# Moving a light feed-forward layer from the second stage of a decoder kernel into its routing iterations

## The reference, cut to what matters

```python
x = x + attn(layernorm(x))
x = x + xattn(layernorm(x), ctx)
n = layernorm(x)                                    # xn3 in the kernel
light = gelu(rms_norm(n) * gamma_l @ w1_l + b1_l) @ w2_l + b2_l      # 512 -> 256 -> 512
s = n @ routing_token
b = -relu(s)
for _ in range(50):                                 # one chain of small steps
    a = 0.1 * log(8) - 0.1 * logsumexp((s + b) / 0.1)
    b = -relu(s + a)
scores = exp((s + a + b) / 0.1);  idx = top_k(scores, 512)
heavy[idx] = gelu(rms_norm(n[idx]) * gamma_h @ w1_h + b1_h) @ w2_h + b2_h   # 512 -> 2048 -> 512
x = x + light + heavy
```

## Time and profile before

| | |
|---|---|
| median of 3 runs | 4434.32 us (4433.23 to 4436.21) |
| profiled execution | 4434.12 us, its span 4432.4 us |
| mean granted TensorE clock | 0.957 of full speed |
| busy, share of the span | PE 92%, DVE 55%, ACT 47%, POOL 60% |
| first stage | ends at about 3104 us |
| second stage | 3104 to 4004 us |
| third stage | 4004 us to the end; routing iterations 4012 to 4122 us |

### The profile page before, as it was taken

One profiled execution on the slowest core, in us unless ns is written; L12 is line 12 of the kernel. 1 busy time (PEld: TensorE's weight loads), 2 busy tenths in 40 slices (PEclk: granted clock), 3 DMA queues, 4 the chain that ended last, 5 costly groups with the idle time before them and its releaser, 6 DMA issues. The chain is left out here.

```text
span 4432.4 us, 59161 instructions
## 1 busy us (share of the span) xinstructions
PE 4057.6 (92%) x18676; PEld 2174.1 (49%) x18676; DVE 2456.1 (55%) x3293; ACT 2075.7 (47%) x3407; POOL 2676.4 (60%) x1343
## 2 busy tenths in 40 slices
PE   8969999999999999999999999997589888883599
PEld 6734444444444444444444444443466666662244
DVE  3336666666666666666666666662266666652400
ACT  2214555655555555555555555554244444441110
POOL 1006888888888888888888888888222222220100
PEclk9968999999999999999999999999799999995799
DMA  6521322322222342122223223220311111112100
GB/s 193 151 68 52 79 57 55 97 57 52 84 71 55 112 116 57 53 82 72 55 55 97 57 52 91 62 53 20 112 51 54 47 55 52 47 33 89 38 10 10
DMA packets 340399, 299.90 MB, mean 68 GB/s; under 512 B 188779, under 2 KB 230251, under 8 KB 339304
## 3 DMA queue, kind: packets, MB, share of 16 engines
q1 hardware_dynamic: 272360, 275.94, 21.9%
q10 hardware_dynamic: 66048, 16.78, 1.7%
q0 software_dynamic: 1920, 6.29, 0.5%
HBM read 117.71 MB, written 64.54 MB: 41 GB/s over the span
## 5 line engine op out<-in xcount | busy, mean ns | idle before, releaser
L239 POOL TENSOR_TENSOR acc<-acc,probs 128x1024 f32<-128x1024 f32 x896 | 2132.4, 2380 | 312.7 <-ACT probs L642 179.7
L729 DVE TENSOR_REDUCE maxes<-ps 128x1 f32<-128x1024 f32 x1024 | 1250.8, 1221 | 709.0 <-PE ps L465 704.1
L645 ACT ACTIVATE probs<-ps,far_bias 128x1024 f32<-128x1024 f32 (+7 forms) x1280 | 1020.4, 820 | 989.0 <-DVE near_s L746 519.2
L500 PE MATMUL ps<-probs,v_head 128*64 128x512 f32 x4096 | 994.6, 606 | 2.3 <-ACT ctx_out L628 2.2
L465 PE MATMUL ps<-stacks 64*128 64x512 f32 x2048 | 761.1, 452 | 33.3 <-DVE maxes L729 32.0
L480 PE MATMUL ps<-stacks 64*128 64x512 f32 x1792 | 671.4, 449 | 0.0
L479 PE MATMUL ps<-stacks 128*128 128x512 f32 x2048 | 625.5, 419 | 2.9 <-ACT probs L642 2.2
L480 PEld LDWEIGHTS ps<-stacks 64*128 64x128 f32 x1792 | 271.7, 184 | 528.7 <-issue 367.2
L500 PEld LDWEIGHTS ps<-probs,v_head 128*64 128x64 f32 x4096 | 248.7, 136 | 483.8 <-issue 480.1
L479 PEld LDWEIGHTS ps<-stacks 128*128 128x128 f32 x2048 | 347.7, 188 | 228.5 <-issue 163.6
L746 DVE TENSOR_TENSOR near_s<-ps,near_bias 128x384 f32<-128x384 f32 (+2 forms) x576 | 285.0, 495 | 284.8 <-PE ps L480 261.6
(11 more groups left out here) (221 smaller groups left out, 4967.4 us busy)
## 6 DMA issues: line engine op xcount, KB each, us to landing
stacks<-c_k SPq DMA_DIRECT2D x128, 256.0 KB, 2.4
stacks<-c_q SPq DMA_DIRECT2D x128, 256.0 KB, 2.6
stacks<-c_d SPq DMA_DIRECT2D x256, 128.0 KB, 2.5
scr_v<-c_k ACTq DMA_DIRECT2D x32, 512.0 KB, 3.9
stacks<-c_q SPq DMA_DIRECT2D x128, 128.0 KB, 2.5
v_head<-scr_v SPq DMA_DIRECT2D x32, 512.0 KB, 3.7
sums<-scr_inv SPq DMA_DIRECT2D x128, 128.0 KB, 2.9
scr_ctx<-ctx_out SPq DMA_DIRECT2D x128, 128.0 KB, 2.3
```

Of the source, the lines that this page charges most:

```text
L239: pool.tensor_tensor(acc[:, qb, :], acc[:, qb, :], pr, ALU.add).then_inc(s["summed"], 1)
L500: mm = pe.matmul(ps[64 * half:64 * half + 64, PV, :], v_head[:, side, kt, :], probs[:, st % PT_RING, half * 512:(half + 1) * 512], start=k ...
L645: ins = act.activation(probs[:, st % PT_RING, a:z], sc[:, a:z], ACT.Exp, bias=bias)
L729: dve.tensor_reduce(maxes[:, qt, pair:pair + 1], ps[:, MX:MX + 2, :], AX.XY, ALU.max).then_inc(s["max_done"], 1)
```

## The change

The light layer leaves the second stage. Instead of multiplying, that stage transposes `r3`, splits it into a rounded part `t3_hi` (ACT) and a rest `t3_lo` (DVE), and stores both, and `xb`, to scratch. Banks of PSUM are assigned anew. The work on a tile is spread over four iterations in another way: the layernorm `xn3`, the dot product, the squares and `r3` move from `here(2)` to `here(3)` and stand first on DVE, ahead of `x1` of the newest tile; on PE the output projection comes first, then the transposed probabilities, then the scores; on ACT the squares come first and `ctx_hi` is computed one tile ahead; on POOL `sq2` comes first, then `ctx_lo` one tile ahead, then the two other powers, each followed at once by its `xb`. The first 8 iterations are written out (before, 4), then 5 laps of four in a `Fori`, then 7 more.

In the third stage the 50 iterations are written out without a loop. From iteration 3 on, PE issues 8 fp32r matmuls of the light layer's first product behind the matmul of each iteration (192 in all: 8 chunks of 512 tokens, 2 halves of the hidden width, 12 terms each), and DVE copies each finished half to SBUF between `dif` and `total`. After iteration 26, ACT runs 16 Gelus of 128x512 in one go. From there PE makes the second product of one tile per iteration (four tiles at once behind iteration 26), two fp32 matmuls of 512 columns, and DVE adds `xb` in the next iteration; the last 5 tiles go into the levels of the search. POOL prepares the light weights at the start of the stage. SP loads the chunks of t3 into two buffers of 2 MB, the xb tiles into four, and stores the output tiles. `hidden` shares its memory with the heavy `w2`, which is therefore loaded after the last tile. The scratch tensor is `(2, P, KT, NB * S)` in fp32. The diff, cut to its core:

```diff
-def middle(nc, io, scr, out):
+def middle(nc, io, scr):
...
-        TP, WO, PV, W1, TURN, WO2, Q2, W2, ROWS = 3, 5, 6, 7, 6, 5, 7, 6, 5
+        TP, WO, PV, TURN, WO2, Q2, ROWS = 3, 5, 6, 7, 4, 7, 3
...
-            for j in range(AGES):
-                iteration(j, j, lambda age, j=j: age <= j)
-            with engine.Fori(1, NBLK) as i:
+            for j in range(2 * TB):
+                iteration(j, j % TB, lambda age, j=j: age <= j, True)
+            with engine.Fori(2, NBLK - 1) as i:
                 for a in range(TB):
-                    iteration(i * TB + a, a, lambda age: True)
-            for j in range(NTILES, NTILES + AGES - 1):
-                iteration(j, j % TB, lambda age, j=j: j - age < NTILES)
+                    iteration(i * TB + a, a, lambda age: True, True)
+            for j in range(NTILES - TB, NTILES + AGES - 1):
...
+                if here(3):
+                    sp.wait_ge(s["r3"], j - 2)
+                    sp.dma_start(scr_r3[j - 3], r3[:, other, :]).then_inc(s["r3_stored"][other], 16)
+                    if a == 2:
+                        sp.dma_start(scr["s"][(j - 6) // TB], sdot[:]).then_inc(s["s_stored"], 16)
+                    sp.wait_ge(s["xb2"], j - 2)
+                if more and (not isinstance(j, int) or j > 0):
+                    sp.dma_start(x[:, (a + 1) % 4, :], rows_in[j + 1]).then_inc(s["x_in"][other], 16)
+                if here(3):
+                    sp.wait_ge(s["t3_lo"], j - 2)
+                    sp.dma_start(scr_t3[0, j - 3], t3_hi[:, other, :, :].bitcast(F32)).then_inc(s["t3_stored"][other], 16)
+                    sp.dma_start(scr_t3[1, j - 3], t3_lo[:, other, :, :].bitcast(F32)).then_inc(s["t3_stored"][other], 16)
                 if here(2):
-                    sp.wait_ge(s["r3"], j - 1)
-                    sp.dma_start(scr_r3[j - 2], r3[:, side, :]).then_inc(s["r3_stored"][side], 16)
-                    if a == 1:
-
-                        sp.dma_start(scr["s"][(j - 5) // TB], sdot[:]).then_inc(s["s_stored"], 16)
...
+            def iteration(j, a, here, more):
+                if here(3):
+                    pool.wait_ge(s["sq1"], j - 2)
+                    pool.tensor_tensor(sq[:, 1:2], sq[:, 1:2], expo[:], ALU.pow).then_inc(s["sq2"], 1)
+                if more:
...
-                    for m in range(LM):
-                        for k in range(KT):
-                            mm = pe.matmul(ps[:, W1, m * P:(m + 1) * P], w1[:, k, m * P:(m + 1) * P], turned3[:, k, :], start=k == 0, stop=k == KT - 1)
-                    mm.then_inc(s["gmm"], 1)
...
-                    for k in range(LM):
-                        mm = pe.matmul(ps[:, W2, :], gelu[:, k, :], w2[:, k, :], start=k == 0, stop=k == LM - 1)
-                    mm.then_inc(s["ymm"], 1)
...
+            def iteration(j, a, here, more):
+                et = e[:, 1 - a % 2, :, :]
+                out, ring_3 = 1 - a % 2, (a + 1) % 4
+                if here(3):
+                    dve.wait_ge(s["pw2"], j - 2)
+                    dve.tensor_scalar(xn3[:, out, :], x[:, ring_3, :], mom[:, 1, 0:1], rs[:, 1:2], ALU.subtract, ALU.mult).then_inc(s["xn3"], 1)
+                    dve.wait_ge(s["xn3"], j - 2)
...
+                if here(3):
+                    dve.wait_ge(s["t3_hi"], j - 2)
+                    dve.tensor_tensor(t3_lo[:, out, :, :], ps[:, ROWS, :].rearrange("p (k n) -> p k n", n=P),
+                                      t3_hi[:, out, :, :].bitcast(F32), ALU.subtract).then_inc(s["t3_lo"], 1)
...
+TOKENS = 512
+NCHUNK = NB * S // TOKENS
+HIDDEN_TERMS = [(k, part, w) for k in range(KT) for part, w in ((0, 0), (0, 1), (1, 0))]
+HIDDEN = [(ch, m, at) for ch in range(NCHUNK) for m in range(LM) for at in range(len(HIDDEN_TERMS))]
+HIDDEN_FROM, HIDDEN_STEP = 3, 8
+HIDDEN_TO = HIDDEN_FROM + len(HIDDEN) // HIDDEN_STEP
+GELU_AFTER = HIDDEN_TO - 1
+EARLY_ROWS = 4
+def hidden_of(i):
+    first = (i - HIDDEN_FROM) * HIDDEN_STEP
+    return HIDDEN[max(first, 0):max(first + HIDDEN_STEP, 0)]
+def hidden_done(i):
+    last = len(HIDDEN_TERMS) - 1
+    return [ch * LM + m for ch, m, at in hidden_of(i) if at == last]
+def light_of(i):
+    if i == GELU_AFTER:
+        return list(range(EARLY_ROWS))
+    tile = EARLY_ROWS + i - HIDDEN_TO
+    return [tile] if i >= HIDDEN_TO else []
+LIGHT_IN_LOOP = EARLY_ROWS + N_ITERS - HIDDEN_TO
...
+            for ch in range(2):
+                tokens_in(ch)
+            for j in range(4):
+                xb_in(j)
...
+            for ch in range(2, NCHUNK):
+                sp.wait_ge(s["hidden_mm"], LM * (ch - 1))
+                tokens_in(ch)
+            for j in range(NTILES):
+                sp.wait_ge(s["light"], j + 1)
+                sp.dma_start(out_tiles[j], light[:, j % 4, :]).then_inc(s["light_stored"][j % 4], 16)
+                if j + 4 < NTILES:
+                    xb_in(j + 4)
+            sp.dma_start(w2[:], io["w2h"]).then_inc(s["w2_in"], 16)
...
+            pool.wait_ge(s["light_in"], N_LIGHT)
+            for k in range(KT):
+                ins = pool.tensor_scalar(wl1[:, k, :], wl1[:, k, :], gamma_l[:, k:k + 1], None, ALU.mult)
+            ins.then_inc(s["wl1"], 1)
+            pool.wait_ge(s["wl1"], 1)
+            pool.tensor_copy(wl1_hi[:], wl1).then_inc(s["wl1_hi"], 1)
+            pool.wait_ge(s["wl1_hi"], 1)
...
+            def hidden_mm(ch, m, at):
+                q = ch * LM + m
+                if at == 0:
+                    if m == 0:
+                        pe.wait_ge(s["t3_in"][ch % 2], 32 * (ch // 2 + 1))
+                    if q == 0:
+                        pe.wait_ge(s["wl1_lo"], 1)
+                    if q >= 3:
+                        pe.wait_ge(s["hidden"], q - 2)
+                k, part, w = HIDDEN_TERMS[at]
+                mm = pe.matmul(ps[:, 1 + q % 3, :], (wl1_hi, wl1_lo)[w][:, k, m * P:(m + 1) * P], t3[:, ch % 2, part, k, :],
+                               start=at == 0, stop=at == len(HIDDEN_TERMS) - 1)
+                if at == len(HIDDEN_TERMS) - 1:
+                    mm.then_inc(s["hidden_mm"], 1)
+            def light_mm(j):
+                pe.wait_ge(s["gelu_l"], LM * (j // 4 + 1))
+                if j >= 4:
+                    pe.wait_ge(s["light"], j - 3)
+                for k in range(LM):
+                    mm = pe.matmul(ps[:, 4 + j % 4, :], hidden[:, k, j * P:(j + 1) * P], wl2[:, k, :], start=k == 0, stop=k == LM - 1)
+                mm.then_inc(s["light_mm"], 1)
+            for i in range(N_ITERS):
+                pe.wait_ge(s["ex"], i + 1)
+                pe.matmul(ps[:, 0, 0:NB * NT], ones[:], ex[:].rearrange("p b t -> p (b t)"), start=True, stop=True).then_inc(s["mm"], 1)
+                for ch, m, at in hidden_of(i):
+                    hidden_mm(ch, m, at)
+                for j in light_of(i):
+                    light_mm(j)
...
+                if i == GELU_AFTER:
+                    act.wait_ge(s["light_in"], N_LIGHT)
+                    for q in range(NCHUNK * LM):
+                        part = hidden[:, q % LM, q // LM * TOKENS:(q // LM + 1) * TOKENS]
+                        act.wait_ge(s["hidden"], q + 1)
+                        act.activation(part, part, ACT.Gelu, bias=bl1[:, q % LM:q % LM + 1]).then_inc(s["gelu_l"], 1)
...
+            def hidden_out(q):
+                dve.wait_ge(s["hidden_mm"], q + 1)
+                dve.tensor_copy(hidden[:, q % LM, q // LM * TOKENS:(q // LM + 1) * TOKENS], ps[:, 1 + q % 3, :]).then_inc(s["hidden"], 1)
+            def light_out(j):
+                dve.wait_ge(s["light_mm"], j + 1)
+                dve.wait_ge(s["xb_in"][j % 4], 16 * (j // 4 + 1))
+                if j >= 4:
+                    dve.wait_ge(s["light_stored"][j % 4], 16 * (j // 4))
+                dve.tensor_tensor(light[:, j % 4, :], ps[:, 4 + j % 4, :], xb[:, j % 4, :], ALU.add).then_inc(s["light"], 1)
+            for i in range(N_ITERS):
+                dve.tensor_tensor(low[:], s_max[:], neg_a[:].unsqueeze(2).to_broadcast([P, NB, NT + 1]), ALU.min).then_inc(s["low"], 1)
+                dve.wait_ge(s["low"], i + 1)
+                dve.tensor_tensor(dif[:], low[:, :, 0:NT], spread(low[:, :, NT]), ALU.subtract).then_inc(s["dif"], 1)
+                for q in hidden_done(i - 1):
+                    hidden_out(q)
+                for j in light_of(i - 1):
+                    light_out(j)
+                dve.wait_ge(s["mm"], i + 1)
```

More of the change, by code:

```diff
@@ L862, in middle @@
         r3 = sb("r3", [P, 2, D])
-        turned1, turned3 = sb("turned1", [P, KT, P]), sb("turned3", [P, KT, P])
+        turned1 = sb("turned1", [P, KT, P])
+        t3_hi, t3_lo = (sb(n, [P, 2, KT, P], F32R) for n in ("t3_hi", "t3_lo"))
         q2 = sb("q2", [P, CM, P])
@@ L881, in middle @@
         scores_ps = ps[:, 0:3, :].rearrange("p a n -> p (a n)")[:, 0:CH * CL]
-        TP, WO, PV, W1, TURN, WO2, Q2, W2, ROWS = 3, 5, 6, 7, 6, 5, 7, 6, 5
+        TP, WO, PV, TURN, WO2, Q2, ROWS = 3, 5, 6, 7, 4, 7, 3
```

(50 more changed lines are left out.)

289 lines of the change are left out of this document (129 added, 160 removed).

## The result

4301.28 us median of four runs (4298.64 to 4305.69) against 4433.84 (4433.23 to 4436.21): ratio 0.970, 95% interval 0.9687 to 0.9714. That is 132.6 us less. 153 were forecast; 4301 lies in the range given (4252 to 4332), but 3 us above what the likeliest case allowed itself (4264 to 4298). The profiled execution took 4298.64 us, its span is 4296.5.

The account below looks back on a forecast made before the run. Stage two was taken as bound by PE or a loop through it, then narrowly by DVE; routing by chain latency. 4434.1 - 184.5 (stage two) + 31 (stage three) = 4281 us, own range 4264 to 4298, wider range 4252 to 4332.

Parts of the forecast that it names:

- the likeliest case: Whole kernel: the main forecast of 4281 us, own range 4264 to 4298, given a chance of 0.60.
- stage two, start: First to fourth x1: output projection no longer stands behind scores and softmax; 54 us instead of 76.0, -22.
- stage two, 28 tiles: Steady tiles: 19.6 us each instead of 25.28, plus 0.5 for each of five back edges; -156.5 us.
- stage two, end: Last x1 to the next stage: 59 us, with 3 for a lower PE clock, instead of 65.1; -6.
- iterations 0 to 2: Stage three's first routing iterations: 6.2 us, plus 3 because POOL's weight preparation blocks low and dif; 9.2.
- iterations 3 to 26: Hidden light matmuls: PE bounds at 2.2 us each, 52.8, plus 2 for the clock and 10.7 for chunks; 65.5 us.
- burst: After iteration 26: 16 Gelus, 10 us, and two table loads of 1.28, less 1.5 of overlap; 11 us.
- iterations 27 to 49: Second light product: light_out stands ahead of total, so 2.33 us per iteration; 53.6 us.
- ahead of the loop and behind it: Stage three: start before routing unchanged; behind the loop light_out, last tile and waits, less 2.7 by clock; +1 us.
- The rival: Stage two: ctx_lo gets the port ahead of r3, +1.9 us per tile, 28 tiles, 4334 us; chance 0.12.
- the 10.7: Iterations 3 to 26: chunk waits, 6.7 us from having two buffers and 4 from chunk 2 standing behind the weights.
- The second rival: Stage three dearer: slower chunks, two taking 21.6 us, +17, or light iterations dragged to 2.7, +8; 4306 us; chance 0.14.

Follow-up runs that it names:

- e3: The changed kernel with the second stage's loop over five blocks of four tiles written out, leaving no back edge: 4291.40 us.
- e5: The changed kernel with VectorE's r3 always waiting until GpSimd's ctx_lo of the next tile is done: 4356.41 us.
- e10: The changed kernel with a third buffer for the light layer's token chunks, so each load starts one chunk earlier: 4292.38 us.
- e4: The changed kernel with the loads of w1 and the other weights put behind the light layer's token chunks on SyncE's queue: 4303.09 us.
- e2: The changed kernel with the light layer's first weight prepared by ScalarE and VectorE instead of GpSimd: 4299.04 us.
- e11: The changed kernel with light weights prepared on ScalarE and VectorE and w1's load behind the token chunks: 4296.08 us.
- e7: The changed kernel with GpSimd's preparation of the light weights put ahead of its all-reduce: 4306.56 us.
- e1: The changed kernel with the table set for both Exp and Ln loaded once more right behind the Gelus: 4283.39 us.

## Why the prediction came out as it did

| term | forecast | measured |
|---|---|---|
| stage two, start | -22 | -23.2 from first to fourth x1; the first x1 itself 3.1 earlier |
| stage two, 28 tiles | -156.5 | -158.0 |
| stage two, end | -6 | -3.9 |
| iterations 0 to 2 | 9.2 | 6.2 |
| iterations 3 to 26 | 65.5 | 74.0 |
| burst | 11 | 12.2 |
| iterations 27 to 49 | 53.6 | 69.3 |
| ahead of the loop and behind it | +1 | -0.4 |

(Stage three by the Ln starts: 16.08 - 9.88; 87.99 - 16.08 and one ordinary iteration of 2.07; 14.27 - 2.07; 67.25 and 2.07 for the last one. The last row is what is left of the 52.3 us over the kernel before, with 109 us for its loop.)

**Right.** VectorE's chain bounds the second stage. The sum of its spacings gave 19.2, with 0.4 for ctx_lo 19.6, and a pass without a jump behind it takes 19.3 in the mean. The mean over all is 19.64, and that it comes so near is luck: the 0.4 us that every pass should lose to ctx_lo came out smaller, and the back edge cost 2.3 us at four jumps (e3: 9.9 us) where 0.5 in five stood. The forecast had the margin of 0.15 us between r3 and ctx_lo (0.16 measured) and called the passes very regular; it had the delay of a back edge too, in another term of the sum, and didn't put the two side by side. The rival's tile time, 19.6 + 1.9 = 21.5 us, is what e5 measures: 21.50 in the mean of 28 passes.

**Right by its size alone.** The hidden iterations: 2.15 us each (2.2), and chunks that stall. The intervals before the Ln of iterations 10, 16 and 22 take 9.5 us more than the 1.84 each that they take with a third buffer (e10); 10.7 were forecast. The forecast's 15.9 us for two chunks became 15.2 (iterations 9 to 15) and 16.6 (15 to 21). The place was not wholly that of the forecast: no chunk waited behind w1 (e4), because the weights were late first; take that away and chunk 2 does (e2, e11). The buffers were the cause (e10), by the arithmetic given: two chunks need a landing and the use of one chunk, one after the other. So the 10.7 came out nearly right because the buffers cost more than their 6.7, and w1 cost nothing of its 4.

**Wrong: "POOL prepares the light weights meanwhile, some 6 us".** The work is 7.0 us, but it starts 18.5 us into the stage. Nothing of it disturbs low and dif (0 instead of 3 us in iterations 0 to 2); instead iteration 3 takes 14.01 us instead of 2.2, 11.8 more than the forecast had there. What GpSimd does in the 10.34 us between the all-reduce and the next operation no run shows; e7 shows that it is tied to that order. The trace of before had the 6.9 us ahead of the all-reduce in view, as part of the 8.3 us to the first routing step, but no operation behind it.

**Wrong, and the largest: "burst: ... two table loads of 1.28"** and the 2.33 per iteration after it. There were 48: one ahead of the Gelus, one for each Exp and each Ln of the 23 iterations behind them, and one for the exponential of the scores. The second of the two was taken to bring back the set that serves both; e1 shows that it does so only where the kernel asks for it. 17.9 us, more than four fifths of the 21 that were missing. The second rival's number, 4306, is nearer to the time measured than the forecast is, but what it gave as the reasons for a dearer third stage didn't come: two chunks took 15.2 and 16.6 us and not 21.6, and the light iterations were drawn out by the loads and not by DVE or the xb transfers. The Trainium skill ("ScalarE: Activation LUTs", "Table sets: the hidden batching unit") says that Ln and then Exp need one load, as one set has both. This trace agrees ahead of the burst and in e1, and disagrees behind the burst, where no set was named: two loads of 1.28 us in each iteration. The same page ("What ACT_TABLE_LOAD costs") would have a switch cost about 2.7 us, load and drain; here the Exp starts 1.29 us after the start of its load (3915.37 to 3916.66).

The clue was in sight: the change's one line that names a set stands at the head of the stage, ahead of iteration 0, and nothing like it behind the Gelus.
